# Cross attention with layer norms: transposes of the softmax parts moved, the prologue's roots shortened, one vector added by accumulating transfers

## What is computed

```python
text_p = x @ W_text + b_text
audio_p = ctx @ W_audio + b_audio
Q = layer_norm(text_p, g1, beta1)
K = layer_norm(audio_p, g2, beta2)
alpha = softmax(Q @ K.T / sqrt(512))
H = (alpha @ audio_p) @ W_out + b_out
return layer_norm(H + x, g_out, beta_out)      # (..) * rsqrt(var + 1e-5) * g_out + beta_out
```

## Time and profile before

| | |
|---|---|
| median of 3 runs | 279.62 us (279.6 to 282.35) |
| the profiled execution | 279.68 us |
| its span, first to last instruction | 277.9 us |
| lies around the span | 1.8 us |
| prologue, up to the first transposes of parts | 63.7 us |
| 30 periods of the steps | 198.5 us, 6.62 us each |
| behind the last of them | 15.7 us |

### The profile page before, as it was taken

One profiled execution on the slowest core, in us unless ns is written; L12 is line 12 of the kernel. 1 busy time (PEld: TensorE's weight loads), 2 busy tenths in 40 slices (PEclk: granted clock), 3 DMA queues, 4 the chain that ended last, 5 costly groups with the idle time before them and its releaser, 6 DMA issues.

```text
span 277.9 us, 5960 instructions
## 1 busy us (share of the span) xinstructions
PE 261.8 (94%) x1671; PEld 231.9 (83%) x1671; DVE 241.2 (87%) x721; ACT 204.0 (73%) x519; POOL 209.2 (75%) x233
## 2 busy tenths in 40 slices
PE   7978999999999999999999999999999999999970
PEld 6757888898989999989998999899989889999830
DVE  3786668978999999999999999999999999999895
ACT  3971339325787788888888788888888887888981
POOL 6081460011379999999999999999999999999985
PEclk9997999999999999999999999999999999999998
DMA  6905059643224444444545444445444444443216
GB/s 189 329 19 178 2 166 368 226 128 106 78 79 151 152 154 151 152 156 161 161 161 184 170 172 157 156 154 162 164 165 152 152 151 151 151 153 136 97 68 264
DMA packets 19456, 43.25 MB, mean 156 GB/s; under 512 B 2050, under 2 KB 2382, under 8 KB 19434
## 3 DMA queue, kind: packets, MB, share of 16 engines
q1 hardware_dynamic: 18810, 41.96, 44.3%
q10 hardware_dynamic: 624, 1.06, 1.2%
HBM read 21.19 MB, written 16.78 MB: 137 GB/s over the span
## 4 chain that ended last, share of the span: by engine, by line
PE 51%; DVE 31%; issue 9%; ACT 3%; POOL 3%; ACTq 1%; POOLq 0%; DVEq 0%
PE psY L1333 13%; PE psY L1344 10%; DVE waste_dve L964 6%; PE psE L1312 5%; PE psO L1356 5%; DVE x_lo L862 5%; PE psT L1262 4%; DVE xs L962 3%; PE psY L1337 3%; DVE hid L984 3%; DVE logits L993 3%; PE psE L1313 2%; DVE neg_max L996 2%; DVE parts L1006 1%; PE psY L1178 1%
## 5 line engine op out<-in xcount | busy, mean ns | idle before, releaser
L1333 PE MATMUL psY<-proj,x_hi 128*128 128x336 f32 x512 | 102.0, 332 | 0.0
L1333 PEld LDWEIGHTS psY<-proj,x_hi 128*128 128x128 f32 x512 | 79.8, 189 | 0.2
L465 POOL TENSOR_TENSOR zs<-zs,shift 128x512 f32<-128x512 f32 x55 | 70.9, 1288 | 4.3
L459 POOL TENSOR_TENSOR zs<-zs,gain 128x512 f32<-128x512 f32 x55 | 71.0, 1291 | 1.0 <-ACT zs L662 1.0
L471 POOL TENSOR_TENSOR rstd<-stat_eps,neg_half 128x4 f32<-128x4 f32 x30 | 30.5, 1017 | 35.0 <-DVE stat_eps L976 32.2
L651 ACT ACTIVATE waste_act<-hid,xs 128x512 bf16<-128x512 f32 x60 | 43.1, 718 | 12.3 <-DVE hid L984 12.3
L964 DVE CUSTOM_DVE_ANT_0 waste_dve<-psY,xs,sums 128x515 bf16<-128x515 f32 x64 | 48.4, 757 | 2.2
L1344 PE MATMUL psY<-proj,x_lo 128*128 128x336 f32 (+1 forms) x256 | 49.5, 315 | 0.0
L662 ACT ACTIVATE zs<-hid,shift,rstd 128x512 f32<-128x512 f32 x59 | 47.5, 805 | 0.0
L984 DVE SCALAR_TENSOR_TENSOR hid<-psO,inv_sum,xs 128x512 f32<-128x512 f32 x60 | 44.8, 747 | 0.0
L862 DVE TENSOR_TENSOR x_lo<-psT,x_hi 128x512 fp32r<-128x512 f32 x64 | 43.7, 682 | 0.7 <-ACT x_hi L620 0.5
(11 more groups left out here) (270 smaller groups left out, 426.4 us busy)
## 6 DMA issues: line engine op xcount, KB each, us to landing
xs<-in_x_dram SPq DMA_DIRECT2D x64, 256.0 KB, 3.0
out_dram<-zs SPq DMA_DIRECT2D x29, 512.0 KB, 3.8
proj<-proj SPq DMA_DIRECT2D x4, 768.0 KB, 8.9
out_dram<-zs SPq DMA_DIRECT2D x6, 256.0 KB, 2.1
xs<-in_L_xattn_W_text_dram SPq DMA_DIRECT2D x4, 256.0 KB, 3.6
xs<-in_L_xattn_W_out_dram SPq DMA_DIRECT2D x2, 512.0 KB, 5.1
wa<-in_L_xattn_W_audio_dram SPq DMA_DIRECT2D x1, 768.0 KB, 6.9
zs<-in_ctx_dram SPq DMA_DIRECT2D x1, 462.0 KB
```

The lines of the kernel that those rows point to most:

```text
L459: nc.gpsimd.tensor_tensor(zs[:, q, t, :], zs[:, q, t, :], gain[:], ALU.mult).then_inc(zg_ready, 1)
L465: nc.gpsimd.tensor_tensor(zs[:, q, t, :], zs[:, q, t, :], shift[:], ALU.add).then_inc(out_ready, 1)
L1333: nc.tensor.matmul(psY[:, t, to:to + HALF], x_hi[:, par, t, k * P:(k + 1) * P], proj[:, q, k, right * HALF:(right + 1) * HALF], start=(k = ...
```

## The change

Three edits.

1. **TensorE, in every step**: `transpose_prob` is called behind the two left-bank x_lo products, ahead of the four of the right bank, instead of ahead of the last x_hi product.
2. **Prologue**: the squares of W_text's parts 1 and 2 are taken by VectorE as dot products, right behind its four `wtT_lo`, those of parts 0 and 3 stay with ScalarE; the chain to `gram_left` comes ahead of the sums of b_text; `root_cols` has 4 columns and is written by 2 instructions instead of 6, ahead of `keys_lo` and `linear`; the minus sign is made where the transposed rows are copied out. TensorE transposes the roots between `audio_product(1)` and `(2)` and does `less_root(0)` ahead of `gram(1)`.
3. **beta_out**: GpSimd no longer adds shift by two instructions per step. Behind both gains of a body it issues one transfer of its own queue, which adds shift to a whole step in `zs` (128 x 2 x 512), SBUF to SBUF, accumulating. SyncE's store waits for that transfer to land (`shifted`). This holds for 28 steps; the last steps keep instructions.

```diff
-        root_cols = sb("root_cols", [P, KD, 6], F32R)
+        root_cols = sb("root_cols", [P, KD, 4], F32R)
...
-                    wait_if_positive(sp, out_ready, T, i, T * (b - 6) + T)
+                    sp.wait_ge(shifted[q], 16 * (j + 1))
...
-            def shift_of(b, i, t, lag):
+            def shift_by_dma(b, i, lag):
 
                 q = (b - lag) % B
-                wait_if_positive(pool, zg_ready, T, i, T * (b - lag) + t + 1)
-                nc.gpsimd.tensor_tensor(zs[:, q, t, :], zs[:, q, t, :], shift[:], ALU.add).then_inc(out_ready, 1)
+                wait_if_positive(pool, zg_ready, T, i, T * (b - lag) + T)
+                pool.dma_start(zs[:, q, :, :], shift[:].rearrange("p (a h) -> p a h", a=1).to_broadcast([P, T, H]),
+                               accum_op=ALU.add).then_inc(shifted[q], 16)
...
                 if live(5):
                     gain_of(b, i, 1, 5)
-                    shift_of(b, i, 1, 5)
                 if live(4):
                     gain_of(b, i, 0, 4)
-                    shift_of(b, i, 0, 4)
+                if live(5):
+                    shift_by_dma(b, i, 5)
...
-            for k in range(1, KD):
-                gram_square(k)
+            act.wait_ge(gram_sq_ready, 1)
+            gram_square(KD - 1)
...
+            for k in (1, 2):
+                nc.vector.tensor_tensor_reduce(out=waste_dve[:, k, 0:H], in0=wt[:, k, :], in1=wt[:, k, :], scale=1.0, scalar=0.0,
+                                               op0=ALU.mult, op1=ALU.add, accum_out=gram_diag[:, k:k + 1]).then_inc(gram_dot_ready, 1)
...
-                nc.vector.tensor_copy(root_cols[:, :, 0], root[:]).then_inc(root_cols_ready, 1)
+                nc.vector.tensor_copy(root_cols[:], root[:].rearrange("p (k a) -> p k a", a=1).to_broadcast([P, KD, 4])).then_inc(root_cols_ready, 1)
                 dve.wait_ge(root_cols_ready, 1)
                 nc.vector.tensor_tensor(root_cols[:, :, 2], root[:], f32(root_cols[:, :, 0]), ALU.subtract).then_inc(root_cols_ready, 1)
-                nc.vector.tensor_copy(root_cols[:, :, 1], root[:]).then_inc(root_cols_ready, 1)
-                nc.vector.tensor_scalar(root_cols[:, :, 3], f32(root_cols[:, :, 0]), -1.0, None, ALU.mult).then_inc(root_cols_ready, 1)
...
-            nc.vector.tensor_copy(root_rows[:, 1, :], ROOT_BANK[1][0:3, :]).then_inc(root_rows_ready, 1)
...
+                if k == 1:
+                    dve.wait_ge(root_psum, 1)
+                    nc.vector.tensor_scalar(root_rows[:, 1, :], ROOT_BANK[1][0:3, :], -1.0, None, ALU.mult).then_inc(root_rows_ready, 1)
...
-                    if n == before and between is not None:
-                        between(b, i)
...
                 last.then_inc(projB_psum, 1)
-                if before == 2 * KD and between is not None:
+                if between is not None:
                     between(b, i)
```

More of the change, by code:

```diff
@@ L245, in cross_attention @@
         shift2_ready = sem("shift2_ready")
+        shifted = [sem(f"shifted{b}") for b in range(B)]
         z_ready, zg_ready, out_ready = sem("z_ready"), sem("zg_ready"), sem("out_ready")
@@ L374, in _ @@
             store(LAST - 1, 0, out_tail, 2)
-            store(LAST - 3, None, out_ready, T * (LAST - 3) + T)
+            store(LAST - 3, None, out_ready, T)
             store(LAST - 1, 1, out_tail, 3)
@@ L378, in _ @@
             store(LAST, 1, out_tail, 5)
-            store(LAST - 2, 0, out_ready, T * (LAST - 2) + 1)
+            store(LAST - 2, 0, out_ready, T + 1)
             for b in range(B):
@@ L576, in _ @@
             audio(1)
+            act.wait_ge(root_psum, 2)
+            nc.scalar.activation(root_rows[:, 0, :], ROOT_BANK[0][0:3, :], ACT.Copy).then_inc(root_rows_ready, 1)
             out_hi(1)
@@ L798, in _ @@
                 nc.vector.tensor_tensor(wtT_lo[:, k, :], W_BANK[k], f32(wtT_hi[:, k, :]), ALU.subtract).then_inc(wtT_lo_ready, 1)
+            for k in (1, 2):
+                nc.vector.tensor_tensor_reduce(out=waste_dve[:, k, 0:H], in0=wt[:, k, :], in1=wt[:, k, :], scale=1.0, scalar=0.0,
+                                               op0=ALU.mult, op1=ALU.add, accum_out=gram_diag[:, k:k + 1]).then_inc(gram_dot_ready, 1)
+            dve.wait_ge(gram_sq_ready, 2)
+            dve.wait_ge(gram_dot_ready, 2)
+            nc.vector.tensor_scalar(gram_kept[:], gram_diag[:], KEPT, None, ALU.mult).then_inc(kept_ready, 1)
+            dve.wait_ge(kept_ready, 1)
+            nc.vector.tensor_tensor(gram_left[:], gram_diag[:], f32(gram_kept[:]), ALU.subtract).then_inc(left_ready, 1)
+            dve.wait_ge(left_ready, 1)
+            nc.vector.tensor_scalar(gram_left[:], gram_left[:], 1e-30, None, ALU.max).then_inc(left_ready, 1)
             dve.wait_ge(bt_loaded, 16)
@@ L850, in _ @@
                     linear(k)
-                if k == 0:
-                    root_parts()
-            dve.wait_ge(root_psum, 1)
-            nc.vector.tensor_copy(root_rows[:, 1, :], ROOT_BANK[1][0:3, :]).then_inc(root_rows_ready, 1)
+                if k == 1:
+                    dve.wait_ge(root_psum, 1)
+                    nc.vector.tensor_scalar(root_rows[:, 1, :], ROOT_BANK[1][0:3, :], -1.0, None, ALU.mult).then_inc(root_rows_ready, 1)
             linear(2)
@@ L1191, in _ @@
             audio_product(1)
+            pe.wait_ge(root_cols_ready, 2)
+            for n, bank in ((1, ROOT_BANK[1]), (0, ROOT_BANK[0])):
+                for k in range(KD):
+                    last = nc.tensor.transpose(bank[0:3, k * P:(k + 1) * P], f32(root_cols[:, k, n:n + 3]), ident[:])
+                last.then_inc(root_psum, 1)
             audio_product(2)
@@ L1194, in _ @@
             audio_product(3)
-            pe.wait_ge(root_cols_ready, 6)
-            for n, bank in ((0, ROOT_BANK[1]), (1, ROOT_BANK[0])):
-                for k in range(KD):
-                    last = nc.tensor.transpose(bank[0:3, k * P:(k + 1) * P], f32(root_cols[:, k, 3 * n:3 * n + 3]), ident[:])
-                last.then_inc(root_psum, 1)
+            less_root(0)
             gram(1)
-            less_root(0)
             less_root(1)
@@ L1314, in transpose_prob, with project @@
                 last.then_inc(probT_psum, 1)
-            def project(b, i, t, between=None, before=7):
+            def project(b, i, t, between=None):
                 q, par = (b - 1) % B, (b - 1) % 2
```

23 lines of the change are left out of this document (7 added, 16 removed).

## The result

The changed kernel takes 314.21 us (median of 6 runs, 310.63 to 320.21), the kernel before 279.81 us beside it: a ratio of 1.111 with a 95% interval of 1.104 to 1.118. The forecast was 277.1 us, with a range up to 280.2. It is wrong by 37 us by the medians, and in sign.

The account below looks back on a forecast made before the run. The prediction took the steps to be bound by TensorE and VectorE waiting for each other once per step, period 6.62 us. Prologue -3.8, steps +1.3 and tail -0.1 sum to -2.6 us: 277.1 us, range 273 to 280.2.

Parts of the forecast that it names:

- the part on beta_out: Steps: GpSimd's additions become a transfer landing in 4 us; issue of 1 us and store's wait both hidden, 0 us.
- 1.5 us are to spare: SyncE, each step: the x load behind the store lands at 96.8, its transposes come at 98.3.
- Rival 3: Steps: GpSimd's issue beyond 2.8 us holds up the root, 28 times; at 3.3 us the time is 291; chance 0.1.
- The sentence beside it: Within the slower rival: added traffic delaying a load of x by more than its 1.5 us has the same sign.
- The prologue: Before the steps: roots' transposes lose their stall, `gram(1)` runs at full clock, mean's product at 23.3 instead of 27.11: -3.8 us.
- The case that the dot products are not held: Prologue bound: if `wo_lo` does not hold VectorE's dot products, TensorE does not wait and the gain is 4.4 us.
- The steps: Transposes' new place: a loop of TensorE and ScalarE gives period 6.66 against 6.62, +1.3 us over 30 periods, bounds 0 to +2.5.
- The wait of 0.34 us: TensorE, each step: moves from before the transposes to before the mix, which comes 1.35 us after the transposes.
- Rival 1: Steps become VectorE's: TensorE's loop falls under 6.49 us, 3.9 us less instead of 1.3 more, 272.0 us; chance 0.2.
- Rival 2: Prologue: roots still held because `root_parts` meets `wo_lo`; gain 1 us or less, 280.0 us; chance 0.12.
- Rival 4: Prologue's gain absorbed by a transfer before the first step, change acts in the steps only, 281 us; chance 0.03.
- GpSimd's relief: Steps: 56 GpSimd additions go, 2.6 us of each period; GpSimd is late for nothing, so this alone gives 0.

Follow-up runs that it names:

- f1: The changed kernel with GpSimd's transfer writing shift over `zs` instead of adding it, so the output is beta_out alone in 28 steps: 278.6 us, ratio 0.999.
- f2: The changed kernel with the accumulating transfer cut to tile 0 of a step (256 KB), beta_out left out of tile 1: 279.82 us, ratio 1.0006.
- e4: The changed kernel with SyncE's store one step later (lag 7 instead of 6), behind the loads of x: 280.92 us, ratio 1.005.
- g1: The changed kernel with the accumulating transfer split in two of 256 KB, each issued behind its tile's gain, SyncE's order kept: 281.09 us, ratio 1.009.
- f3: The changed kernel with SyncE's store one step later and the transposes of the parts back at their old place: 280.97 us, ratio 1.002.
- g2: The kernel before with the prologue's edit alone, measured a second time with more rounds: 276.42 us, ratio 0.9929.
- f4: The kernel before with the transposes' new place and the prologue's edit, beta_out still by GpSimd's instructions: 280.56 us, ratio 1.0008.
- e2: The kernel before with the prologue's edit alone: 277.31 us, ratio 0.991.
- e1: The kernel before with the transposes' new place alone: 281.22 us, ratio 1.0025.

## Why the prediction was wrong

**The step that failed** is in the part on beta_out: the landing "I take 4 us", and from it "Hidden: 0". The rest of the working held in outline. It says that the store goes out near the time of the next load of x, that this load stands behind it on SyncE, and that 1.5 us are to spare. With a landing of 3.8 us (f1) or 4.1 us (f2) the result is indeed hidden. The landing was 6.6 us, 2.6 more than taken, and that is more than the 1.5. What was missing is a bound: the 4 us came from a load of half the size, with its 3.0 us, although no row showed an accumulating transfer, and no second end was given. Twice the nearest row, 6 us, would have been past the room. The spare time itself was also counted too high: it leaves out the 0.8 us between the landing and the load's issue, and it has x loads at 3.0 us, which were 3.6 us in the median of the changed kernel and 3.9 to 5.1 in the chain's late ones. The page's rule weighed there (the Trainium skill, "DMA: Bandwidth & Descriptors", anatomy of one DMA) gave 3.2 us. The plain transfer of f1 came near it with 3.8; the accumulating one of the same bytes did not, with 6.6.

**The price of the failure** was not foreseen either. A load that is late by 3 us costs 2.3 us of standing and another 1.6 us behind it, where the granted clock is lower, and something like this in nine of 30 periods, with two short ones after each; why just two was not worked out. The split is read in one execution, whose mean granted clock is 0.938; at a higher clock its part must be smaller, and no trace shows how much.

**Rival 3** had the right sign and was given 0.1, but its mechanism was the wrong one. GpSimd's issue is 1.24 us, near the 1 us taken, and the root never waits for it: the root's own wait is for VectorE, 95.1 us in the page. The sentence beside it has the right consequence, late loads of x, but names the added traffic as their reason; by e4 and g1 it is the store's wait on SyncE. It was given no price of its own, though the working had put the margin at only 1.5 us. It should have been the slower rival: by the prediction's own margin it decides from 5.5 us of landing on, by the count above from 4.7 to 5.3.

**The prologue**, forecast -3.8 us: the first transposes start 3.2 us earlier in the changed kernel, 3.8 in e4, 3.7 in f3, 3.8 in f1, 3.5 in g2 and 4.3 in f4. In the profiled executions that had the lower clock at the start it was 1.3 earlier (e2) or 0.6 to 0.7 later (f2, g1). The mechanism is as written, with two exceptions. VectorE's first two dot products of `linear` were not held by `wo_lo`. They took 0.68 us each, so the rows' copy came at 19.26 instead of 20.6; it was GpSimd that stood, 6.04 us for its four instead of 5.49. The first of them began at 16.90, just ahead of `wo_lo` at 16.91. The third began while the last `wo_lo` ran, and it took 1.21 us:

```profile
22.29 1.21 DVE L834 CUSTOM_DVE_ANT_0 waste_dve<-xs,bt_rows 128x512 bf16<-128x512 f32 x1
```

So in these two places the instruction that began later was the longer one; the prediction took VectorE's to be the held one each time. (The row that it names as agreeing with exclusion, L836, has one SBUF input; L838 beside it, with two, took 1.19 us.) The case that the dot products are not held had its own bound in the forecast, 4.4 us, and f4 comes near it. The other exception is a sum: `gram(1)` was taken at 2.1 us, but 1.59 us for two thirds of the columns make 2.39, and it took 2.38. In the changed kernel's profiled execution TensorE also reached the transposes at 16.68 instead of 16.02, and `less_root(0)` began at 20.76, as forecast, without the stall of 0.4 us. By the ratios the edit gave 2.5 us (e2) and 2.0 us (g2) of measured time.

**The steps**, forecast +1.3 us, bounds 0 to 2.5: +2.3 in e1 and +2.1 in f4. The wait of 0.34 us came out at 0.35 and the 1.35 us to the mix exactly; the mean period was 6.69 us instead of 6.66: in e1 most have 6.68 to 6.70, nearly as counted, and eleven have 6.73 to 6.76. The term was mis-sized by 1 us within its bounds.

**Rivals 1, 2 and 4** did not occur: no period fell to 6.5 us, the roots were not held, and the prologue's gain reached the first step.

**GpSimd's relief** was forecast to give nothing, and gives nothing (f3). Nor was it free: f3 is 2.5 to 3 us above the prologue's edit alone, where the prediction put the transfers at 0.

## What to carry to other kernels

Before work is handed to a DMA queue, write down who waits for the landing and what stands behind that waiter in its queue's order; the room is up to the next thing in that order which somebody needs, and a landing time that no row shows wants a bound on the far side of that room. A store that waits is best placed behind the loads that must not wait, one step later if need be. That takes the loss away and does not make the transfer a gain: here the work it took off GpSimd was not what the steps waited for. Where a transfer is too long for its place, two halves, each issued as soon as its data is there, can fit where the whole does not.

## What the runs showed that was not expected

- An accumulating transfer inside SBUF, 512 KB, lands in 6.6 us (5.0 to 8.4) and in 7.2 us in e4; the same one without accumulation in 3.8; two of 256 KB in 3.7 each. The whole one has nearly twice the packets with accumulation (7616 against 4032 in the queue), each at some 0.2 us of a DMA engine either way.
- GpSimd's issue follows the packets more than the bytes: 0.79 us for the plain 512 KB, 0.91 to 0.94 for the accumulating 256 KB, 1.24 for the accumulating 512 KB.
- TensorE's granted clock fell to 0.62 for 4.5 us behind a stretch in which it was busy for 1.92 of 4.30 us, and a stall of 2.4 us became a loss of 4.0.
